# Key rows loaded from a second DMA queue, and eight row maxima moved to the end of the sequence before

## The chip, the cores and the metric

One Trainium2 chip, one of its cores. The metric is the device time of one execution, in microseconds; the time of the kernel before is the median of three runs. A profile shows one execution: its engines are TensorE (PE, with its weight loads PEld), VectorE (DVE), ScalarE (ACT), GpSimd (POOL), and the sequencers that issue DMAs, SyncE (SP) and ScalarE's (ACTq). 16 DMA engines move the data.

## What is computed

Two transformer layers on an input of 8 sequences of 512 rows of 128. The change lies in the first layer's part, which for each sequence is

```python
x = L0_attn_x
xn = _layernorm(x, axis=-1)
x = x + _L0_attn_ref(xn, ...) + _L0_ffn_ref(xn, ...)
```

where the attention has 16 heads of 8 dimensions, with keys and values from a latent of 32:

```python
q = (x @ W_q).reshape(b, t, N_HEADS, HEAD_DIM).transpose(0, 2, 1, 3)
k = (lat @ W_uk).reshape(b, t, N_HEADS, HEAD_DIM).transpose(0, 2, 1, 3)
v = (lat @ W_uv).reshape(b, t, N_HEADS, HEAD_DIM).transpose(0, 2, 1, 3)
q = apply_rope(q)
k = apply_rope(k)
scores = jnp.einsum('bhqd,bhkd->bhqk', q, k) / jnp.sqrt(jnp.float32(HEAD_DIM))
scores = jnp.where(causal[None, None], scores, -jnp.inf)
attn = jax.nn.softmax(scores, axis=-1)
```

and the FFN is a mixture of 32 experts (hidden 64, the best 4 of them) with a shared expert. The second layer, a gated delta rule with two mixtures of experts, is computed after it for all sequences in a loop of its own.

## The kernel before

Five engine programs are written out by hand and meet at semaphores. The first loop runs 8 times, once a sequence, and computes layer 1; the second runs 8 times for layer 2. The order of the first loop is the list that `schedule_l0` (L97) makes; each engine walks it and emits its own part of each step.

For one sequence the list is: `gu(p)` for p = 0 to 16, the gate and up products of a pair of experts (the 17th is the shared expert; TensorE L540, L543, ScalarE's Silu L973), `hid(p)`, VectorE's two products with the gate and the routing weight (L1361, L1364; `spread`, L532, gives the weight), and `wbd(p)`, the down product (L555). Between them stand the row maxima `max(n)`, n = 0 to 63, one for a head and a tile of 128 queries: TensorE multiplies the query rows with the key rows up to the diagonal (L570, 128 to 512 columns wide, `head_and_tile`, in banks 0 and 2 by turns), and VectorE adds the mask and reduces (L1372, behind a small waiting instruction, L326). n = 0, 1 are 128 wide, 2, 3 256, 4, 5 384, 6, 7 512, and so on in groups of eight. Six of them stand in each of the steps p = 2 and p = 3, four in each of p = 4 to 16. `maxneg` and `maxrows` turn the maxima of each half into rows that are stored, split in three bf16 parts, and loaded beside the query rows.

Then come the scores and exponentials `exp(g, i)` (L592, L597, ScalarE L982), 48 of them, the products with the values `pv(g)` (L610), numerator and denominator `nd` (L621), and `attn_out`: VectorE's reciprocal (L1394) and product (L1396), TensorE's output product (L628), VectorE's residual add, x1 (L1400). In between, the next sequence is prepared: `fnorm`, `fT`, `fq`, `flat`, `flatT`, `fk`, `fv`, `froute`, `fw` compute its normed input, queries, latent, keys, values and routing weights. What is prepared for the first sequence runs once ahead of the loop (`ahead_of_loop`).

Queries and keys are split in three bf16 parts each, stored to DRAM (`scratch_out`, L356, the scratch `scrq` and `scrk`) and loaded again in the layout that the products want (`scratch_in`, L365): the query rows QS and the key rows KS, each by 12 DMAs whose destination is 8 partitions x 8 x 512 bf16, 64 KB. All 24 are issued by SyncE, the queries' first, as soon as TensorE has done the last score of the running sequence, since QS and KS are read until then. TensorE waits for `d_q` and `d_k` ahead of maximum 0 (L565, L566), which stands in step p = 2 of the next sequence, behind gu(0) to gu(2). Behind the 24 loads SyncE stores x1 to `mid` (L396) and loads the next input.

After the loop VectorE waits for the last loads, which nothing uses, and clears XT (L1430); SyncE loads x1 of the first sequence back from `mid` (L401), and the second loop's first statistics start (L1218).

## Time and profile before

| | |
|---|---|
| median of 3 runs | 3121.79 us (3119.16 to 3141.93) |
| profiled execution | 3141.66 us, span 3139.9 us |
| granted TensorE clock, mean | 0.887 of 2.4 GHz |
| busy: PE, PEld, DVE, ACT, POOL | 86%, 58%, 65%, 38%, 12% |
| first loop in the span | about 62 to 1175 us |
| x1 (L1400), first and last of 8 | 216.2 and 1158.3 us |
| DMAs arena<-scrq, arena<-scrk | 108 and 108, 64 KB each |

"Busy" is an engine's share of the span; TensorE's matmuls are pipelined, so their busy time is not peak use. Per sequence the first loop takes 134.6 us ((1158.3-216.2)/7). Windows and timelines below are in us from the span's start; "[idle before <-releaser]" is the time that the engine stood still before the row and what it was released by. "DMA share" is the mean busy share of the 16 DMA engines.

### The profile page before, as it was taken

To read this page: it belongs to the slowest core of one execution; us is meant where nothing else is said; L and a number is where in the kernel's file an instruction comes from. 1 tells how busy PE (TensorE), PEld (TensorE's weight loads), DVE (VectorE), ACT (ScalarE), POOL (GpSimd) and SP (SyncE) were. 2 spreads that over 40 slices of the span, in tenths; PEclk is the share of its full clock that TensorE was granted. 3 is DMA by queue.
4 is the path that set the end of the run, shared out by engine and by line. 5 is a ranking of instruction groups with operands and counts; after the bars stand their busy time and mean duration, and the time that the engine had idled before them with its cause. 6 is when DMAs were issued, how large, how long until landed. Compare 5 with 4: busy or idle time off the path is not lost.

```text
span 3139.9 us, 48523 instructions
## 1 busy us (share of the span) xinstructions
PE 2691.1 (86%) x15020; PEld 1805.5 (58%) x15020; DVE 2042.6 (65%) x6346; ACT 1185.7 (38%) x2170; POOL 382.3 (12%) x284
## 2 busy tenths in 40 slices
PE   2888888888888867997997897898898898898898
PEld 1434343343433425784785685585596595586587
DVE  4757666585766748558558557657656756845845
ACT  0132231313223125445445444444444444544543
POOL 0000000000000002122112122021120220221211
PEclk8888878897898967998998998997998898899799
DMA  5020101102011121101101101101201201100110
GB/s 139 10 38 7 33 14 25 35 5 37 12 28 21 18 51 41 48 11 58 48 11 58 48 11 49 57 8 48 61 1 55 54 8 55 43 19 28 54 34 15
DMA packets 133697, 109.63 MB, mean 35 GB/s; under 512 B 76968, under 2 KB 117488, under 8 KB 132944
## 3 DMA queue, kind: packets, MB, share of 16 engines
q1 hardware_dynamic: 130192, 100.01, 12.7%
q10 hardware_dynamic: 3264, 6.82, 0.6%
q8 instruction: 100, 1.64, 0.2%
q14 instruction: 141, 1.16, 0.1%
HBM read 86.62 MB, written 20.19 MB: 34 GB/s over the span
## 4 chain that ended last, share of the span: by engine, by line
PE 62%; issue 18%; DVE 11%; DMA 3%; ACT 3%; SPq 2%; POOL 1%; DVEq 0%; ACTq 0%; POOLq 0%
PE bank L871 7%; PE bank L881 7%; PE bank L459 5%; DMA arena<-scrk 3%; DVE arena L1519 3%; PE bank L716 2%; PE bank L610 2%; PE bank L737 2%; PE bank L819 2%; PE bank L555 2%; PE bank L782 2%; PE bank L777 2%; PE bank L765 2%; PE bank L540 2%; PE bank L769 2%
## 5 line engine op out<-in xcount | busy, mean ns | idle before, releaser
L881 PEld LDWEIGHTS bank<-wring,arena 128*128 128x128 f32 x2048 | 269.1, 192 | 109.5 <-issue 107.2
L871 PE MATMUL bank<-arena,wring 128*128 128x512 f32 x512 | 294.8, 666 | 25.9 <-ACT arena L1100 25.9
L1100 ACT ACTIVATE arena<-bank,w_b 128x512 f32<-128x512 f32 x256 | 175.1, 687 | 274.2 <-PE bank L871 273.9
L1519 DVE SCALAR_TENSOR_TENSOR arena<-bank,w_convw,arena 128x511 f32<-128x511 f32 (+2 forms) x384 | 254.8, 740 | 34.6 <-ACT arena L1014 34.5
L881 PE MATMUL bank<-wring,arena 128*128 128x128 f32 x2048 | 271.1, 276 | 0.0
L973 ACT ACTIVATE arena<-bank 128x512 f32<-128x512 f32 x136 | 81.4, 599 | 494.7 <-PE bank L540 441.9
L459 PE MATMUL bank<-w_ident,arena 128*128 128x128 f32 (+2 forms) x1164 | 178.5, 293 | 86.4 <-DVE arena L1266 35.7
L1372 DVE CUSTOM_DVE_ANT_0 bank<-bank,arena 128x128 f32<-128x128 f32 (+3 forms) x512 | 249.2, 492 | 0.0
L982 ACT ACTIVATE arena<-bank 128x512 f32<-128x512 f32 (+1 forms) x384 | 171.1, 535 | 148.9 <-PE bank L597 147.1
L459 PEld LDWEIGHTS bank<-w_ident,arena 128*128 128x128 f32 (+2 forms) x1164 | 135.9, 141 | 118.6 <-issue 66.6
L692 PE MATMUL bank<-arena,w_Wqkvz 128*128 128x512 f32 x256 | 152.7, 733 | 45.0 <-DVE arena L1519 26.1
L1066 ACT ACTIVATE arena<-bank 128x512 f32<-128x512 f32 (+1 forms) x256 | 118.7, 488 | 136.2 <-PE bank L777 69.3
L570 PE MATMUL bank<-arena 48*128 48x128 bf16 (+3 forms) x512 | 110.7, 317 | 64.7 <-DVE arena L1372 36.0
L555 PE MATMUL bank<-arena 128*128 128x128 f32 x1088 | 161.7, 293 | 2.7 <-DVE arena L1357 2.7
L1684 DVE SCALAR_TENSOR_TENSOR arena<-bank,arena 128x128 f32<-128x128 f32 x224 | 63.1, 344 | 154.5 <-PE bank L881 152.7
L540 PE MATMUL bank<-arena 128*128 128x512 f32 x272 | 156.3, 659 | 8.1 <-ACT arena L973 8.1
L326 DVE TENSOR_TENSOR tick<-nhalf 128x1 f32<-128x1 f32 x600 | 94.1, 157 | 93.0 <-PE bank L570 86.4
L543 PE MATMUL bank<-arena 128*128 128x512 f32 x272 | 152.2, 644 | 0.0
L570 PEld LDWEIGHTS bank<-arena 48*128 48x128 bf16 x512 | 34.1, 93 | 200.5 <-DVE arena L1372 92.3
L555 PEld LDWEIGHTS bank<-arena 128*128 128x128 f32 x1088 | 135.6, 196 | 22.8 <-issue 11.3
L1175 POOL TENSOR_TENSOR arena<-arena,w_blk 128x512 f32<-128x512 f32 x64 | 79.8, 1268 | 509.5 <-PE bank L765 358.8
L1165 POOL TENSOR_TENSOR arena<-arena 128x512 f32<-128x512 f32 x64 | 92.3, 1475 | 352.2 <-ACT arena L1033 224.6
(273 smaller groups left out, 5209.3 us busy)
## 6 DMA issues: line engine op xcount, KB each, us to landing
wring<-in_w_last SPq DMA_DIRECT2D x64, 512.0 KB, 3.3
arena<-scrg SPq DMA_DIRECT2D x32, 512.0 KB, 5.4
arena<-scrq SPq DMA_DIRECT2D x108, 64.0 KB
arena<-scrk SPq DMA_DIRECT2D x108, 64.0 KB
scrn<-arena SPq DMA_DIRECT2D x64, 64.0 KB, 1.9
arena<-scrn SPq DMA_DIRECT2D x8, 512.0 KB, 3.6
scrx<-arena SPq DMA_DIRECT2D x8, 512.0 KB, 2.6
arena<-scrx SPq DMA_DIRECT2D x64, 64.0 KB, 2.1
```

What stands on the lines that cost most here:

```text
L459: return nc.tensor.transpose(dst, src, W["ident"][0:k, 0:k])
L540: mm(bk[:, :], W["gate0"][:, p, :] if p < PR0 else W["sg"][:], xnT, start=True, stop=True).then_inc(*s["p_gate"].up)
L543: mm(bk[:, :], W["up0"][:, p, :] if p < PR0 else W["su"][:], xnT, start=True, stop=True).then_inc(*s["p_up"].up)
L555: last = mm(bank[7][:, t * P:(t + 1) * P], HID[:, p % 2, t * P:(t + 1) * P], W["down0"][:, p, :] if p < PR0 else W["sd"][:], start=(p == 0 ...
L570: mm(bk[:, 0:w], QS[o:o + KROWS, h // 2, qt * P:(qt + 1) * P], KS[o:o + KROWS, h // 2, 0:w], start=True, stop=True, tile_position=(o, 0)). ...
L692: mm(bk[:, :], W["Wqkvz"][:, m * P:(m + 1) * P], zT, start=True, stop=True).then_inc(*s["p_qkv"].up)
L871: mm(bank[HBANK[f]][:, :], wring[:, e % 2, k * P:(k + 1) * P], xn1T, start=True, stop=True).then_inc(*s["p_fh"].up)
L881: last = mm(bank[OBANK[e]][:, t * P:(t + 1) * P], GH[:, f % 2, t * P:(t + 1) * P], wring[:, e % 2, FC * P + k * D:FC * P + (k + 1) * D], s ...
L982: fn(PT[:, slot, col:col + w], bank[SBANK[n % 4]][:, 0:w], ACT.Exp, scale=float(HD) ** -0.5).then_inc(*s["a_p"].up)
L1100: fn(GH[:, f % 2, :], bank[HBANK[f]][:, :], ACT.Gelu_apprx_tanh, bias=W["b1"][:, f:f + 1]).then_inc(*s["a_gh"].up)
L1372: v.tensor_tensor_reduce(bk[:, 0:w], bk[:, 0:w], W["maskq"][:, S - w:S], 1.0, PAD, ALU.add, ALU.max, mx[:, col:col + 1]).then_inc(*s["v_ma ...
L1519: ins = v.scalar_tensor_tensor(out=cv[:, k:S], in0=bank[2 + m % 4][:, 0:S - k], scalar=W["convw"][:, m, 3 - k:4 - k], in1=cv[:, k:S], op0= ...
```

## The change

It has three parts.

1. `scratch_in` on SyncE issues the 12 query loads only. The 12 key loads go to ScalarE's queue (`keys_in`), in the place of step `nd`, behind its last exponential, with the same waits.
2. Maxima 0 to 7 of the next sequence (`amax`, `AHEAD` = 8) are made at the end of this one: two between VectorE's product for the output and the output product, six behind the residual add. For the first sequence all eight are made ahead of the loop. The waits for `d_q` and `d_k` go with maximum 0, and `attn_out` is cut in two on VectorE (`att`, `attn_out`).
3. The other 56 maxima stand four in each of steps p = 2 to 15, from n = 8; the steps p = 2 and 3 have two fewer, p = 16 has none.

```diff
-    order, n = [("gu", 0)], 0
+    order, n = [("gu", 0)], AHEAD
     for p in range(1, PR0 + 1):
-        many = 0 if p == 1 else 6 if p in (2, 3) else 4
+        many = 0 if p in (1, PR0) else 4
...
-    order += [("pv", NQ - 1), ("nd",), ("attn_out",)]
+    order += [("pv", NQ - 1), ("nd",), ("att",), ("amax", 0), ("amax", 1), ("attn_out",)] + [("amax", i) for i in range(2, AHEAD)]
...
-                for name, scr, dst, kinds in (("q", scrq, QS, QSPLIT), ("k", scrk, KS, KSPLIT)):
-                    if name == "k":
-                        sp_.wait_ge(*s["d_scrk"].at(b, 32, k))
-                    for hh in range(2):
-                        for t, kind in enumerate(kinds):
...
+                for hh in range(2):
+                    for t, kind in enumerate(QSPLIT):
+                        rows = 64 * hh + HD * t
+                        sp_.dma_start(QS[rows:rows + HD, :, :], rows_of(scrq, kind, hh)).then_inc(*s["d_q"].up16)
...
+            def amax(b, k, n):
+
+                h, qt = head_and_tile(n)
+                o, w = 64 * (h % 2), P * (qt + 1)
+                if n == 0:
+                    pe.wait_ge(*s["d_q"].at(b, 16 * 12, k))
+                    pe.wait_ge(*s["d_k"].at(b, 16 * 12, k))
+                if k and n < 2:
+                    pe.wait_ge(*(s["v_os"].at(b, NQ), s["v_rden"].at(b, 1))[n])
+                if n >= 2:
+                    pe.wait_ge(*s["v_max"].at(b, n - 1, k))
+                mm(bank[(0, 2)[n % 2]][:, 0:w], QS[o:o + KROWS, h // 2, qt * P:(qt + 1) * P], KS[o:o + KROWS, h // 2, 0:w],
+                   start=True, stop=True, tile_position=(o, 0)).then_inc(*s["p_max"].up)
...
+            def keys_in(b, k):
+                if k:
+                    act.wait_ge(*s["p_score"].at(b, 12 * NQ))
+                act.wait_ge(*s["d_scrk"].at(b, 32, k))
+                for hh in range(2):
+                    for t, kind in enumerate(KSPLIT):
+                        rows = 64 * hh + HD * t
+                        act.dma_start(KS[rows:rows + HD, :, :], rows_of(scrk, kind, hh)).then_inc(*s["d_k"].up16)
...
+                         "nd": lambda: keys_in(b, 1)}
```

TensorE's rows where one sequence ends. Before, from the last products of `nd` (L621) over the output product (L628) to the loop's branch:

```order
L621 MATMUL bank<-arena 32x512 [waits v_os]
L621 MATMUL bank<-arena 32x512 x4
L628 MATMUL bank<-arena 128x128 [waits v_att]
L628 MATMUL bank<-arena 128x128 x3
L511 REGISTER_ALU
L511 COMPARE_AND_BRANCH
```

and, behind gu(0) and gu(1), the end of the wait's old place in the next turn of the loop, from gu(2) (L540, L543) to maximum 0 (L570):

```order
L540 MATMUL bank<-arena 128x512 [waits a_sg]
L516 ISA
L543 MATMUL bank<-arena 128x512 [waits v_t]
L565 ISA
L567 REGISTER_ALU [waits d_k,d_q]
L570 MATMUL bank<-arena 128x128 [waits v_att,v_os]
```

Now, with `nd` at L639, the maxima of `amax` at L524 and the output product at L646:

```order
L639 MATMUL bank<-arena 32x512 x4
L518 ISA
L524 MATMUL bank<-arena 128x128 [waits v_os,d_k,d_q]
L524 MATMUL bank<-arena 128x128 [waits v_rden]
L646 MATMUL bank<-arena 128x128 [waits v_att]
L646 MATMUL bank<-arena 128x128 x3
L523 REGISTER_ALU
L524 MATMUL bank<-arena 128x256 [waits v_max]
```

The wait for the loaded rows has moved from behind gu(2) of the next sequence to ahead of the output product, and six more maxima stand between that product and gu(0).

VectorE's rows there. Before, the reciprocal, the product, the residual add and the next sequence's first `hid` (L1361):

```order
L1394 RECIPROCAL arena<-bank 128x512 [waits p_nd]
L1258 REGISTER_ALU
L1395 REGISTER_ALU [waits v_tlink]
L1396 TENSOR_TENSOR arena<-bank,arena 128x512 [waits p_nd]
L1399 REGISTER_ALU [waits a_xr,p_acc]
L1400 TENSOR_TENSOR x<-arena,bank 128x512 [waits d_mid]
```

Now, with the same product at L1437, the maxima at L1380 and the residual add at L1443:

```order
L1437 TENSOR_TENSOR arena<-bank,arena 128x512 [waits p_nd]
L331 ISA
L332 TENSOR_TENSOR tick<-nhalf 128x1 [waits p_max]
L1380 ISA bank,arena<-bank,arena 128x128
L1380 ISA arena 128x1
L331 REGISTER_ALU
L332 TENSOR_TENSOR tick<-nhalf 128x1 [waits p_max]
L1380 ISA bank,arena<-bank,arena 128x128
L1380 ISA arena 128x1
L1442 REGISTER_ALU [waits a_xr,p_acc]
L1443 TENSOR_TENSOR x<-arena,bank 128x512 [waits d_mid]
L331 REGISTER_ALU
```

Two maxima have come ahead of the residual add, six stand behind it.

SyncE's rows at the same place, before:

```order
L376 DMA arena<-scrq 8x8x512 [waits p_score]
L376 DMA arena<-scrq 8x8x512 x11
L370 REGISTER_ALU
L376 DMA arena<-scrk 8x8x512 [waits d_scrk]
L376 DMA arena<-scrk 8x8x512 x11
L396 ISA [waits v_x1]
L396 DMA mid<-x 128x4x128
```

and now:

```order
L372 DMA scrk<-arena 128x512 [waits d_scrq]
L376 ISA
L380 DMA arena<-scrq 8x8x512 [waits p_score]
L380 DMA arena<-scrq 8x8x512 x11
L399 ISA [waits v_x1]
L399 DMA mid<-x 128x4x128
```

The key loads have left this queue; they are issued from ScalarE's, and the store to `mid` stands directly behind the query loads.

## Rows read from the trace of the kernel before

**Rows 1.** Who waited for whom, 62 to 1175 us: total, times, longest

```profile
PE bank L570 <- DMA arena<-scrk: 19.1, 5, 12.5
DVE arena L1430 <- issue: 10.5, 1, 10.5
```

**Rows 2.** Timeline, end of the fourth sequence: start, duration, engine, line

```profile
467.47 4.13 SPq L376 DMA_DIRECT2D arena<-scrq  x12
471.71 5.90 SPq L376 DMA_DIRECT2D arena<-scrk  x12
...
480.61 1.90 PE L628 MATMUL bank<-arena 128*128 128x128 f32 x8 [3.41 <-DVE arena L1396]
...
482.63 0.69 DVE L1400 TENSOR_TENSOR x<-arena,bank 128x512 f32<-128x512 f32 x1 [2.08 <-PE bank L628]
...
483.36 0.63 ACT L962 ACTIVATE arena<-arena 128x512 f32<-128x512 f32 x1 [15.01 <-DVE x L1400]
...
484.49 1.28 ACT L973 ACT_TABLE_LOAD   x1
...
486.44 1.13 PE L540 MATMUL bank<-arena 128*128 128x512 f32 x2 [1.29 <-ACT arena L973]
...
488.69 1.02 PE L540 MATMUL bank<-arena 128*128 128x512 f32 x2
...
493.55 0.23 PE L570 MATMUL bank<-arena 48*128 48x128 bf16 x2 [2.97 <-DMA arena<-scrk]
...
497.34 1.91 PE L540 MATMUL bank<-arena 128*128 128x512 f32 x2
```

**Rows 3.** Stretches: length, busy by engine, PEclk, DMA share, GB/s last

```profile
335.00:346.00 11.00, 8.20 (x80) 2.52 (x72) 4.18 (x3) 0.17 (x1) 0.00 (x0) 0.89 0.56 85
468.50:481.00 12.50, 8.27 (x78) 2.75 (x71) 5.43 (x4) 0.00 (x0) 0.00 (x0) 0.91 0.57 71
484.00:488.00 4.00, 2.71 (x7) 1.08 (x6) 0.69 (x1) 2.75 (x4) 0.00 (x0) 0.97 0.95 126
3.00:11.00 8.00, 0.00 (x0) 0.00 (x0) 0.00 (x0) 0.00 (x0) 0.00 (x0) 1.00 1.01 403
...
468.00:469.00 1.00, 1.00 (x8) 0.20 (x4) 0.00 (x0) 0.35 (x2) 0.00 (x0) 0.50 0.35 100
```

**Rows 4.** Timeline of VectorE, maxima of the fifth sequence

```profile
495.55 0.43 DVE L1372 CUSTOM_DVE_ANT_0 bank<-bank,arena 128x256 f32<-128x256 f32 x1
...
497.25 0.56 DVE L1372 CUSTOM_DVE_ANT_0 bank<-bank,arena 128x384 f32<-128x384 f32 x1
```

**Rows 5.** Timeline of TensorE, gate products of gu(2), gu(4), gu(5), gu(6)

```profile
355.47 1.02 PE L540 MATMUL bank<-arena 128*128 128x512 f32 x2
...
365.37 1.02 PE L540 MATMUL bank<-arena 128*128 128x512 f32 x2
...
369.39 1.02 PE L540 MATMUL bank<-arena 128*128 128x512 f32 x2
...
372.90 1.02 PE L540 MATMUL bank<-arena 128*128 128x512 f32 x2
```

**Rows 6.** Timeline of TensorE, first and last down product of a sequence's end

```profile
420.43 1.16 PE L555 MATMUL bank<-arena 128*128 128x128 f32 x8
...
424.43 1.16 PE L555 MATMUL bank<-arena 128*128 128x128 f32 x8 [0.34 <-DVE arena L1357]
```

**Rows 7.** Timeline, first sequence: SyncE's query loads, TensorE's gu(4)

```profile
61.50 4.25 SPq L376 DMA_DIRECT2D arena<-scrq  x12
...
98.78 1.02 PE L540 MATMUL bank<-arena 128*128 128x512 f32 x2
```

**Rows 8.** Timeline of VectorE, end of the first loop

```profile
1158.26 0.69 DVE L1400 TENSOR_TENSOR x<-arena,bank 128x512 f32<-128x512 f32 x1 [1.94 <-PE bank L628]
...
1169.49 3.47 DVE L1430 MEMSET arena<- 128x4096 f32 x1 [10.54 <-issue]
...
1173.02 0.80 DVE L1218 BATCH_NORM_STATS2 stats<-x 128x6 f32<-128x128 f32 x4
```

More of the change, by code:

```diff
@@ L192, in sig @@
             if first:
-                signals[name] = Signal(name, signals[first].sem, per.get(name, 1), (LOOPS + (first in FRONT)) * per.get(first, 1))
+                signals[name] = Signal(name, signals[first].sem, per.get(name, 1), (LOOPS + (first in FRONT)) * per.get(first, 1) + PARTLY.get(first, 0))
             else:
@@ L508, in fw, with first_maxima @@
                 last.then_inc(*s["p_w0T"].up)
-            ahead_of_loop(fT, fq, flat, flatT, fk, fv, fw)
+            def amax(b, k, n):
[10 more added lines that the diff above has]
+                   start=True, stop=True, tile_position=(o, 0)).then_inc(*s["p_max"].up)
+            def first_maxima(b, k):
+                for n in range(AHEAD):
+                    amax(b, k, n)
+            ahead_of_loop(fT, fq, flat, flatT, fk, fv, fw, first_maxima)
             with pe.Fori(0, LOOPS) as b:
@@ L563, in smax @@
                     o, w = 64 * (h % 2), P * (qt + 1)
-                    if n == 0:
-                        pe.wait_ge(*s["d_q"].at(b, 16 * 12))
-                        pe.wait_ge(*s["d_k"].at(b, 16 * 12))
+                    if n == AHEAD:
                         pe.wait_ge(*s["v_os"].at(b, 0))
-                        pe.wait_ge(*s["v_att"].at(b, 0))
-                    bk = after(*(("v_nmt", 1) if n == 32 else ("v_max", max(n - 1, 0))), (0, 2)[n % 2])
+                    bk = after(*(("v_nmt", 1) if n == 32 else ("v_max", n - 1)), (0, 2)[n % 2])
                     mm(bk[:, 0:w], QS[o:o + KROWS, h // 2, qt * P:(qt + 1) * P], KS[o:o + KROWS, h // 2, 0:w],
@@ L634, in _ @@
                          "attn_out": attn_out, "fT": later(fT), "fq": later(fq), "flat": later(flat), "flatT": later(flatT),
-                         "fk": later(fk), "fv": later(fv), "fw": later(fw)}
+                         "fk": later(fk), "fv": later(fv), "fw": later(fw), "amax": lambda n: amax(b, 1, n)}
                 for step in L0:
@@ L982, in expo @@
                     fn(PT[:, slot, col:col + w], bank[SBANK[n % 4]][:, 0:w], ACT.Exp, scale=float(HD) ** -0.5).then_inc(*s["a_p"].up)
-                steps = {"gu": gu, "exp": expo, "fT": lambda: fT(b, 1), "flatT": lambda: flatT(b, 1)}
+                steps = {"gu": gu, "exp": expo, "fT": lambda: fT(b, 1), "flatT": lambda: flatT(b, 1),
+                         "nd": lambda: keys_in(b, 1)}
                 for step in L0:
@@ L1345, in _, with row_max, amax, first_maxima @@
             ahead_of_loop(fnorm, fq, flat, flatT, fk, froute, fw)
+            def row_max(n):
+                h, qt = head_and_tile(n)
+                w, col = P * (qt + 1), h * NT + qt
+                bk = bank[(0, 2)[n % 2]]
+                v.tensor_tensor_reduce(bk[:, 0:w], bk[:, 0:w], W["maskq"][:, S - w:S], 1.0, PAD,
+                                       ALU.add, ALU.max, mx[:, col:col + 1]).then_inc(*s["v_max"].up)
+            def amax(b, k, n):
+                wait_alone(dve, *s["p_max"].at(b, n + 1, k))
+                row_max(n)
+            def first_maxima(b, k):
+                for n in range(AHEAD):
+                    amax(b, k, n)
             def dve_steps(b, k):
@@ L1367, in smax @@
                 def smax(n):
-                    h, qt = head_and_tile(n)
-                    w, col = P * (qt + 1), h * NT + qt
                     wait_alone(dve, *s["p_max"].at(b, n + 1, k))
-                    bk = bank[(0, 2)[n % 2]]
-                    v.tensor_tensor_reduce(bk[:, 0:w], bk[:, 0:w], W["maskq"][:, S - w:S], 1.0, PAD,
-                                           ALU.add, ALU.max, mx[:, col:col + 1]).then_inc(*s["v_max"].up)
+                    row_max(n)
                 def maxneg(half):
@@ L1403, in dve_steps @@
                 later = lambda part: lambda: part(b, k + 1)
[L1404 to L1405 removed]
+                return {"hid": hid, "max": smax, "maxneg": maxneg, "maxrows": maxrows, "pv": pv, "att": attend, "attn_out": attn_out,
+                        "amax": lambda n: amax(b, k + 1, n), "fnorm": later(fnorm), "fq": later(fq), "flat": later(flat), "flatT": later(flatT), "fk": later(fk),
                         "froute": later(froute), "fw": later(fw)}
```

25 lines of the change are left out of this document (12 added, 13 removed).

## Prediction

> **What bounds the kernel now.** I read the views in this order: who waited for whom over the first loop, then one end of a sequence as a timeline, then the DMA share there, then the pace of the steps that the change shortens.
>
> The second loop is untouched and only shifts. In the first loop, which runs from about 62 to 1175 us of the span, TensorE is paced by itself, by VectorE and by three fixed chains. Only 19.1 us of its time wait for key rows, 12.5 of them once, ahead of the first sequence, and 6.6 in four of the seven others [rows 1]. VectorE waits another 10.5 us for the last, unused keys after the loop [rows 1]. So 29.6 us in all is what the loads cost openly. They take much longer than that. In the fourth sequence's end SyncE issues 12 query loads from 467.47 (call this moment S), then 12 key loads from 471.71, and the first maximum starts at 493.55, S+26.1, after 2.97 us of waiting [rows 2]. Everything TensorE does between 480.61 and about 490 (the output product, the first gate and up products of the next sequence, gu(0) to gu(2)) lies over these loads.
>
> Issue is not what takes the time: the 24 issues are over at 477.6, 16 us before the data is there [rows 2]. The loads run at a steady 71 GB/s here and 85 GB/s in another sequence, at a DMA share of 0.57 and 0.56, that is about nine of sixteen engines' worth [rows 3]. When the next input and the stored result join on the same queue, the share goes to 0.95 and the rate to 126 GB/s; the start of the kernel shows 403 GB/s at a share of 1.01 [rows 3]. So there are engines left over that these loads don't use, and each load that is in flight is slow.
>
> **The change part by part.** Call L the landing of the last key row, counted from S. Everything turns on L, because the wait for it moves from ahead of the old first maximum (about S+23 to S+26) to ahead of the output product, which starts at 480.61, S+13.1, now [rows 2].
>
> 1. *What now stands behind the wait.* New order on TensorE: maxima 0 and 1, output product, maxima 2 to 7, then gu(0). The matmuls of maxima 0 and 1 take 0.2 and their wake 0.1, the output product 1.9 [rows 2], so it ends at L+2.2. VectorE then does the residual add, 0.69 [rows 2], and the maxima: one 256 wide is 0.41 after the one before, one 384 wide 0.55, and the 512 wide ones 0.69 each by the same rate per column (an estimate from the 0.43 and 0.56 of the rows), with a gap of about 0.3 at each change of width (an estimate from 495.55 and 497.25, which lie 1.7 apart where three maxima take 1.4) [rows 4]. The six maxima behind the add are 3.3 us of VectorE and 0.7 of such gaps, 4.0: it is through at L+7.1. TensorE needs maximum 5 for the last matmul, about L+5.5, and gu(0) follows. ScalarE's two copies and its table load (1.28) [rows 2] run in that time. gu(0), its activation of 0.6 and the start of gu(1) are at L+7.8, where before gu(1) came 3.9 after the output product's end, at 486.44 [rows 2]. gu(2) follows 2.3 later: L+10.1, against 488.69, S+21.2. Cost of this part: L-11.1.
>
> 2. *What the FFN steps give back.* Before, the two steps after gu(2) hold six maxima each and take 9.9 us where nothing waits (355.47 to 365.37); a step with four wide ones takes 4.0, one with four narrow ones 3.5 [rows 5]. Now all fourteen steps hold four, which makes these two 7.5: 2.4 gained. On top goes the open wait for keys, 6.6/7 = 0.95 a sequence, and what follows it: after the idle time the clock is granted at half and the next product takes 1.91 instead of 1.02 [rows 2]; I put 0.75 on that. The last step now has no maxima: the three down products, 1.16 each, can run back to back instead of ending at 425.6 after starting at 420.43; with the small transpose that is 3.8 instead of 5.2 plus 0.5 that maxnegs and waits add: 1.9 gained [rows 6]. Sum: 2.4+0.95+0.75+1.9 = 6.0.
>
> 3. *Between two sequences*, seven times: L-11.1-6.0 = L-17.1.
>
> 4. *The first sequence.* Query loads are issued at 61.50, the keys need their store landed and start about 2 us later instead of 4. The eight maxima stand alone, 4.2 to gu(0), then 4.8 to gu(2) and 7.5 to gu(4): 61.5+(L+1)+16.5 against 98.78 [rows 7]; and 1.9 less at the last step.
>
> 5. *The end of the loop.* VectorE clears XT (3.47) once the maxima are through: the statistics start at L+10.8 in place of 1173.02. The x1 of that sequence is at 1158.26, which is S+15.2 there, so S is about 1143.1 and the old value S+29.9 [rows 8].
>
> ScalarE's 12 issues cost nothing: it idles 15.01 us ahead of the copy that follows x1, and at SyncE's pace of 5.9 us for twelve [rows 2] they are over by S+7. Without that cover they would cost these 6 us. SyncE has nothing else queued until x1. The banks of maxima 0 and 1 are free before the output product could start, so they hold nothing up.
>
> *How large is L?* No row shows two queues on such loads. 24 loads of 64 KB are 1.57 MB. **If a second queue adds nothing**, 85 to 71 GB/s give 18.5 to 22.2 us, and the packets begin about 1.1 after S (the microsecond from 468 has them only in its second half, at a share of 0.35) [rows 3]: L = 19.6 to 23.3. **If it doubles the rate**, the loads are in by S+13.1 and the output product waits for nothing: L = 13.1. I take 90 GB/s, a little over the best that one queue shows, nearer to the lower end because the share of 0.57 says that the engines which serve these loads are busy all the time: L = 18.6.
>
> Sum at L = 18.6: 7 x 1.5 = +10.5; first sequence 97.6-98.78-1.9 = -3.1; end 29.4-29.9 = -0.5. Together +7 us. On the profiled execution (3141.66 us, span 3139.9) that is 3149; on the median of the runs, 3121.79, it is 3129. The profiled run is 20 us above that median; the difference is not the loads', and I forecast the median.
>
> The Trainium skill (DMA: Bandwidth & Descriptors, "Issuing engines are not separate DMA queues") says that DMAs from several engines run on the same 16 DMA engines and interleave, and that only issue time is saved. By it the time would be that of the rival "nothing gained" below. The same skill (SBUF, "Door 1: The DMA port swizzle") has eight neighbouring partitions behind two of sixteen ports; by that, query rows and key rows in flight on different ports could run side by side, which speaks for the rival "doubled".
>
> **The rivals.**
>
> *Nothing gained (slower).* The wait of L = 19.6 to 23.3 now stands ahead of the output product and all of gu(0) to gu(2), 10 us of TensorE's work that lay over it. For: the share of 0.57 is unchanged between the 71 and the 85 GB/s sequence, so the serving engines look full. Against: their rate differs by a fifth between sequences, so they are not at a hard limit. Price: at 19.6, 17.5-2.1+0.5 = +16; at 23.3, 43.4+1.6+4.2 = +49: 3138 to 3171. It decides on slower at all from L = 17.1, and on slower by 1% from L = 21.2.
>
> *Doubled (faster).* L = 13.1: 7 x -4.0 = -28; first sequence 92.1-98.78-1.9 = -8.6; end -6.0: -43, 3079. For: sixteen engines carry 403 GB/s, these loads 71. At L = 14.2 it is still -32.
>
> *Shared in part*, my forecast: L from 14.2 to 19.6, 3090 to 3138.
>
> A fourth, that ScalarE's issues delay its copies, I leave at 2 in 100: they would have to take 10 us longer.
>
> **How the numbers follow.** Shared in part 0.41, nothing gained 0.33, doubled 0.24, else 0.02. One per cent, 31 us, is about what a measurement of this kernel can tell from no change. Faster by over 1% needs L under 14.2: the doubled case and a little, 0.26. Slower by over 1% needs L over 21.2: most of the second, 0.27. Within: 0.47. The range 3082 to 3168 leaves a tenth out at each end; the likeliest case alone is 3090 to 3138.
>
> **What the profile would show.** L: the idle time of the first maximum's matmul, put down to the key rows, now ahead of the output product; with L = 18.6 it is 5.4 us a sequence. The rate in the first 15 us after S: 71 to 85 GB/s for nothing gained, 140 for doubled. gu(1) 5.6 after the output product. The steps 4.0 and 3.5 from gu(2) on. The forecast falls if the output product still starts at S+13, or if the rate stays at 71.

## The result, and the profile after

| | before | after |
|---|---|---|
| median of four runs each, same chip | 3126.78 us | 3179.93 us |
| ratio, 95% interval | | 1.017 (1.012 to 1.0219) |
| profiled execution, span | 3139.9 us | 3174.5 us |
| second loop's first statistics start | 1173.02 us | 1224.54 us |
| from one sequence's query loads to the next's, mean of seven | 134.6 us | 141.3 us |

The changed kernel is slower by 53 us, and its median lies 12 us above the upper end of the range (3168). The forecast was 3129. The first loop alone holds the loss: the second loop's statistics start 51.5 us later than in [rows 8]. The spans of the two profiled executions lie only 34.6 us apart because the second loop, which is the same in both, took 17 us more in the execution of before. Over the thirteen kernels told of here the time from VectorE's clearing of XT to the end runs from 1954 to 1977 us with the same code, so for the first loop I compare its end and use the ratios for the whole.

The page of the changed kernel, its busy times, the chain that ended last, and the group of the early maxima:

```profile
PE 2647.2 (83%) x15028; PEld 1788.4 (56%) x15028; DVE 2045.4 (64%) x6370; ACT 1184.4 (37%) x2170; POOL 382.0 (12%) x284
...
PE 60%; issue 18%; DVE 10%; DMA 6%; ACT 3%; POOL 2%; SPq 1%; DVEq 0%; ACTq 0%; POOLq 0%
```

Its waits in the first loop, 62 to 1230 us (total, times, longest): ScalarE for x1, TensorE at the first early maximum, VectorE for the early maxima, and TensorE there once more:

```profile
ACT arena L990 <- DVE x L1443: 182.8, 7, 26.7
...
PE bank L524 <- DMA arena<-scrq: 116.1, 8, 15.8
DVE tick L332 <- PE bank L524: 107.1, 24, 12.8
...
PE bank L524 <- DMA arena<-scrk: 15.9, 1, 15.9
```

TensorE stood 19.1 us at the key rows in [rows 1]. Now it stands 132.0 us at the loaded rows (116.1 + 15.9), nine times, the longest 15.9. (Eight of the waits are put down to the query loads. The profile names the transfer that came last by its reckoning, and in the eight loads inside the loop queries and keys land within 0.4 us of each other. In the first load, ahead of the loop, the keys are 5.2 us behind.) DMA is 6% of the chain.

The same end of the fourth sequence as in [rows 2], as a timeline of the changed kernel:

```profile
483.79 4.12 SPq L380 DMA_DIRECT2D arena<-scrq  x12
...
483.88 0.27 ACTq L984 DMA_DIRECT2D arena<-scrk  x1
...
484.18 3.93 ACTq L984 DMA_DIRECT2D arena<-scrk  x11
...
506.41 0.29 PE L524 MATMUL bank<-arena 48*128 48x128 bf16 x2 [13.05 <-DMA arena<-scrq]
506.63 2.07 PE L646 MATMUL bank<-arena 128*128 128x128 f32 x8
...
508.83 0.69 DVE L1443 TENSOR_TENSOR x<-arena,bank 128x512 f32<-128x512 f32 x1 [1.41 <-PE bank L646]
...
509.55 0.63 ACT L990 ACTIVATE arena<-arena 128x512 f32<-128x512 f32 x1 [25.00 <-DVE x L1443]
...
512.55 2.04 PE L561 MATMUL bank<-arena 128*128 128x512 f32 x2
...
516.09 1.63 PE L561 MATMUL bank<-arena 128*128 128x512 f32 x2
...
518.85 1.02 PE L561 MATMUL bank<-arena 128*128 128x512 f32 x2
522.36 1.02 PE L561 MATMUL bank<-arena 128*128 128x512 f32 x2
526.39 1.03 PE L561 MATMUL bank<-arena 128*128 128x512 f32 x2
```

S is 483.79. Both queues have issued their twelve loads by S+4.3 instead of S+10.1, and still the first maximum starts at S+22.6. TensorE stands idle for 13.05 us, from S+9.6 to S+22.6. Before, it stood idle for the first 3.41 us of that and ran the output product and gu(0) to gu(2) in the rest. Stretches of the changed kernel in two sequences, and behind the wait (length, busy by engine, PEclk, DMA share, GB/s):

```profile
486.00:504.00 18.00, 6.53 (x72) 2.07 (x64) 5.43 (x4) 0.00 (x0) 0.00 (x0) 0.78 0.57 77
345.00:363.00 18.00, 5.30 (x56) 1.52 (x48) 5.44 (x4) 0.00 (x0) 0.00 (x0) 0.74 0.57 71
...
506.00:519.00 13.00, 11.13 (x27) 5.29 (x28) 5.82 (x27) 3.60 (x5) 0.00 (x0) 0.57 0.14 40
```

The DMA share with two queues is 0.57, the number of [rows 3] with one, and the rate is 77 and 71 GB/s. The last row is what comes behind the idle time: TensorE is granted 0.57 of its 2.4 GHz on average, so much of the stretch is at the lower level of 1.2 GHz, and gu(0) takes 2.04 where it takes 1.02 at full clock.

### The profile page after: what moved, and what is told of

It reads as the page before. It is cut to its first block, busy times and chain, and to the rows that moved or that the text cites. A ratio compares the mean times of both kernels' runs of the same rounds, so it can differ in the third digit from the quotient of the medians.

```text
span 3174.5 us, 48555 instructions
## 1 busy us (share of the span) xinstructions
PE 2647.2 (83%) x15028; PEld 1788.4 (56%) x15028; DVE 2045.4 (64%) x6370; ACT 1184.4 (37%) x2170; POOL 382.0 (12%) x284
## 3 DMA queue, kind: packets, MB, share of 16 engines
q1 hardware_dynamic: 122416, 92.93, 10.8%
## 4 chain that ended last, share of the span: by engine, by line
PE 60%; issue 18%; DVE 10%; DMA 6%; ACT 3%; POOL 2%; SPq 1%; DVEq 0%; ACTq 0%; POOLq 0%
PE bank L889 7%; PE bank L899 7%; DMA arena<-scrq 5%; PE bank L462 4%; DVE arena L1562 4%; PE bank L561 3%; PE bank L564 2%; PE bank L837 2%; PE bank L576 2%; PE bank L755 2%; PE bank L800 2%; PE bank L795 2%; PE bank L783 2%; PE bank L787 2%; PE bank L856 2%
## 5 line engine op out<-in xcount | busy, mean ns | idle before, releaser
L1562 DVE SCALAR_TENSOR_TENSOR arena<-bank,w_convw,arena 128x511 f32<-128x511 f32 (+2 forms) x384 | 253.9, 736 | 25.0 <-ACT arena L1043 21.6
L1380 DVE CUSTOM_DVE_ANT_0 bank<-bank,arena 128x128 f32<-128x128 f32 (+3 forms) x520 | 253.1, 492 | 0.0
L462 PE MATMUL bank<-w_ident,arena 128*128 128x128 f32 (+2 forms) x1164 | 172.0, 286 | 74.3 <-DVE arena L1295 35.5
L710 PE MATMUL bank<-arena,w_Wqkvz 128*128 128x512 f32 x256 | 148.9, 719 | 43.7 <-DVE arena L1562 26.1
L524 PE MATMUL bank<-arena 48*128 48x128 bf16 (+3 forms) x72 | 25.0, 442 | 144.3 <-DMA arena<-scrq 116.1
L576 PEld LDWEIGHTS bank<-arena 128*128 128x128 f32 x1088 | 133.9, 194 | 18.6 <-issue 12.1
L1043 ACT ACTIVATE arena<-bank,w_convw 128x512 f32<-128x512 f32 x128 | 87.6, 685 | 107.8 <-PE bank L710 107.4
```

The lines of the kernel that those rows point to most:

```text
L462: return nc.tensor.transpose(dst, src, W["ident"][0:k, 0:k])
L576: last = mm(bank[7][:, t * P:(t + 1) * P], HID[:, p % 2, t * P:(t + 1) * P], W["down0"][:, p, :] if p < PR0 else W["sd"][:], start=(p == 0 ...
L710: mm(bk[:, :], W["Wqkvz"][:, m * P:(m + 1) * P], zT, start=True, stop=True).then_inc(*s["p_qkv"].up)
L1380: v.tensor_tensor_reduce(bk[:, 0:w], bk[:, 0:w], W["maskq"][:, S - w:S], 1.0, PAD, ALU.add, ALU.max, mx[:, col:col + 1]).then_inc(*s["v_ma ...
L1562: ins = v.scalar_tensor_tensor(out=cv[:, k:S], in0=bank[2 + m % 4][:, 0:S - k], scalar=W["convw"][:, m, 3 - k:4 - k], in1=cv[:, k:S], op0= ...
```

## The experiments

L is, as in the prediction, the landing of the last key row counted from the issue of the first query load. It is worked out for each of the nine loads of a kernel from the issue rows and the landing times in the trace. "Spacing" is the mean distance from one S to the next over the seven inner sequences; "clear" is the start of VectorE's clearing of XT at the end of the first loop. The ratios are to the kernel before on the same chip, with their 95% intervals.

| kernel | L of the first, of the others | spacing | clear | ratio |
|---|---|---|---|---|
| before | 26.1, 21.7 to 25.7 | 134.6 | 1169.5 | 1 |
| changed | 22.8, 22.5 to 24.2 | 141.3 | 1221.0 | 1.017 (1.012 to 1.0219) |
| two_queues_old_order | 23.9, 23.6 to 25.4 | 136.6 | 1179.6 | 0.9991 (0.9958 to 1.0024) |
| one_queue | 25.8, 21.6 to 26.3 | 141.4 | 1226.4 | 1.0139 (1.0069 to 1.021) |
| before_wide | 13.0, 12.4 to 13.1 | 133.1 | 1136.9 | 0.9881 (0.982 to 0.9941) |
| after_wide | 12.9, 13.1 to 13.6 | 130.3 | 1126.7 | 0.98 (0.9757 to 0.9843) |
| after_wide_one_queue | 14.2, 12.2 to 13.5 | 130.2 | 1125.5 | 0.9796 (0.9753 to 0.9839) |
| wait_behind | 22.6, 22.2 to 25.7 | 140.5 | 1211.8 | 1.0102 (1.0052 to 1.0152) |
| before_wide_even | 13.5, 11.9 to 13.3 | 133.1 | 1138.4 | 0.9867 (0.9818 to 0.9916) |
| other_half | 27.6, 15.6 to 20.2 | 136.0 | 1183.4 | 0.999 (0.9957 to 1.0022) |
| other_rows | 24.2, 16.5 to 21.9 | 137.0 | 1190.2 | 1.0052 (1.002 to 1.0085) |
| sixteen_rows | 15.4, 16.0 to 16.4 | 133.2 | 1150.2 | 0.9956 (0.9923 to 0.9989) |
| eight_rows | 24.2, 26.0 to 28.1 | 143.9 | 1246.4 | 1.0219 (1.0155 to 1.0284) |

### Which part of the change costs

**two_queues_old_order**: the kernel before, with `keys_in` on ScalarE's queue and nothing else.

```diff
-                for name, scr, dst, kinds in (("q", scrq, QS, QSPLIT), ("k", scrk, KS, KSPLIT)):
+                for name, scr, dst, kinds in (("q", scrq, QS, QSPLIT),):
...
+            ahead_of_loop(fT, flatT, keys_in)
```

> The kernel before, with the key loads on ScalarE's queue and nothing else changed: the wait for them stands behind gu(2) of the next sequence as before. Theory A: the time of the kernel before within 0.5%, 3110 to 3140 us; the last row lands 22 to 24.5 us after the first issue and TensorE's wait ahead of maximum 0 is 10 to 30 us in all. Theory B: slower by over 20 us. A landing at 13 to 17 us would give 3090.

**one_queue**: the changed kernel, with all 24 loads back on SyncE's queue.

```diff
+                sp_.wait_ge(*s["d_scrk"].at(b, 32, k))
+                for hh in range(2):
+                    for t, kind in enumerate(KSPLIT):
+                        rows = 64 * hh + HD * t
+                        sp_.dma_start(KS[rows:rows + HD, :, :], rows_of(scrk, kind, hh)).then_inc(*s["d_k"].up16)
...
-            ahead_of_loop(fT, flatT, keys_in)
+            ahead_of_loop(fT, flatT)
...
```

> The changed kernel, but all 24 loads issued by SyncE again, queries first; the maxima stay where the change put them. Theory A (the landing of the last key row does not depend on the number of queues; moving the wait ahead of the output product is the whole loss): the last row lands 21.7 to 26 us after the first query load's issue as in the kernel before, against 22.5 to 24.2 in the changed one, so the time is that of the changed kernel within 0.5%, about 3170 to 3190 us. Theory B (two queues in lockstep slow each other, and the queue split is part of the loss): faster than the changed kernel by over 20 us, 3150 or less. If the queue split had gained anything, this kernel would be slower than 3190.

The second queue alone changes nothing that can be measured in the ratio (0.9991), and taking it away from the changed kernel changes nothing either (1.0139 and 1.017, intervals that overlap widely). The mean L of the seven inner loads is 23.2 and 24.2 in the old order, 24.0 and 23.7 in the new one, with one queue and with two. So the loss lies in the place of the wait. One thing does not fit as well: in the profiled execution of two_queues_old_order a sequence takes 136.6 us against 134.6, and the first loop ends 10.1 us later, which the ratio does not show. Stretches of one_queue, to be put beside the 77 and 71 GB/s above (the first begins 1.2 us ahead of its S, 487.20; from 488.50 to 504 it is 0.57 and 77):

```profile
486.00:504.00 18.00, 9.58 (x86) 2.94 (x84) 5.75 (x5) 2.04 (x6) 0.00 (x0) 0.81 0.51 70
345.00:363.00 18.00, 7.82 (x80) 2.36 (x72) 5.43 (x4) 0.00 (x0) 0.00 (x0) 0.78 0.57 68
```

In two_queues_old_order TensorE's wait for the keys becomes eight waits and not five, 23.2 us in all against 19.1, because L is 24 to 25 in every sequence and not about 22 in four of them:

```profile
PE bank L568 <- DMA arena<-scrk: 23.2, 8, 10.1
```

### Is the new order bad, or only L too long for it?

**before_wide** and **after_wide**: the kernel before and the changed kernel with another layout in the scratch, 48 rows of 16 heads, so that each tensor comes back in two transfers of 48 partitions instead of twelve of eight. The stores become six a tensor, of 128 KB. Of the edit, the loads of before_wide:

```diff
-                    for hh in range(2):
-                        for t, kind in enumerate(kinds):
-                            rows = 64 * hh + HD * t
-                            part = bass.AP(tensor=scr.tensor, offset=kind * P * S + hh * HD * S,
-                                           ap=[[S, HD], [2 * HD * S, NP], [1, S]])
-                            sp_.dma_start(dst[rows:rows + HD, :, :], part).then_inc(*s["d_" + name].up16)
+                    for hh in range(2):
+                        sp_.dma_start(dst[64 * hh:64 * hh + KROWS, :, :], wide_rows(scr, hh)
+                                      ).then_inc(*s["d_" + name].up16)
...
```

> The kernel before, with a scratch of 48 rows (six parts of eight, three of them stored twice or more) so that each half of QS and KS is loaded by one DMA of 48 partitions, 4 loads in place of 24, all from SyncE; the pieces stay 1 KB and the bytes loaded stay the same, the stores grow from 3 to 12. Both theories E and P: the loads run on all sixteen DMA engines and all ports of a half, the rate is 250 GB/s or more, the last row lands within 6 to 9 us, and no matmul waits for it. Then the 19.1 us of TensorE's waits, some 5 us of half clock behind them and 8 of the 10.5 us at the loop's end go: 3085 to 3100 us. If instead the limit were the memory read (small pieces from one small region), it would still take 20 us and the time would be that of the kernel before.

> The changed kernel with nothing altered but the scratch layout and the load shape: each tensor comes back in 2 transfers of 48 partitions instead of 12 of eight. In the kernel before, this shape brought L (landing of the last key row, counted from the issue of the first query load) down to 12.4 to 13.1 us. By the prediction's own sum with L = 12.7: seven sequences L - 17.1 = -4.4 us each, -31; first sequence about -6; end of loop 23.5 instead of 29.9, -6; together about -43 us against the kernel before, ratio 0.986, and some 5 us under before_wide. Theory A (the change's order is sound and only the load's length spoilt it): ratio 0.984 to 0.988, no wait of more than 2 us on the keys in the loop. Rival B (the order itself costs, whatever the load's length, because eight maxima and the output product now stand in the end of the sequence): slower than before_wide (0.988) by 3 us or more.

For before_wide an L of 6 to 9 us was expected, at 250 GB/s or more. It came to 12.4 to 13.1 us, at 139 GB/s. Still its wait at the maxima is gone but for 1.9 us once, ahead of the first sequence, and every spacing is 133.1. The ratio of after_wide lies where theory A has it, and a little under (0.98 for 0.984 to 0.988), and rival B is out: spacing 130.3, first loop 42.8 us shorter than in the profiled execution of before ("about -43"). TensorE's waits ahead of the early maxima in after_wide, 62 to 1230 us:

```profile
PE bank L528 <- issue: 25.0, 6, 5.3
...
PE bank L528 <- DMA arena<-scrk: 8.9, 1, 8.9
...
PE bank L528 <- DMA arena<-scrq: 7.6, 2, 4.0
```

16.5 us in three pieces are put down to the loads, 8.9 of them once, and the other two are longer than the 2 us that theory A allowed. Those two and the six of 25.0 us stand where the old order had 3.41 of idle time ahead of each output product [rows 2], until VectorE's product is there. In the fourth sequence of after_wide the keys land at S+13.5, 466.8, and the first maximum starts at 466.90; VectorE's product had ended at 466.15. So L is still what releases TensorE, but by 0.7 us there. Over the eight loads of the loop the keys land 0.0 to 0.8 us behind the end of that product, and 1.9 in one, and a shorter L would bring little more than that.

So the order is not bad in itself. With L at 13 it is 2.8 us a sequence better than the old one, with L at 24 it is 6.7 worse. (Over the whole first loop after_wide is 10.2 us ahead of before_wide in the profiled executions, and after_wide_one_queue, below, 11.4; the intervals of the ratios 0.98 and 0.9881 overlap.) after_wide beats both kernels of this study, by 2.0% and 3.6% (0.98/1.017).

The seven spacings are not the whole of it. At the same L the first sequence and the end of the loop cost more in the new order, since nothing lies over the loads there: from the first S to the second it is 127.9 us in after_wide and 123.9 in before_wide, from the last S to the clearing of XT 21.5 and 16.6.

**after_wide_one_queue**: the same four wide loads, all from SyncE.

```diff
+                sp_.wait_ge(*s["d_scrk"].at(b, 96, k))
+                for hh in range(2):
+                    sp_.dma_start(KS[64 * hh:64 * hh + KROWS, :, :], wide_rows(scrk, hh)).then_inc(*s["d_k"].up16)
...
```

> As after_wide, with the four wide loads all from SyncE's queue. If two queues working on the same rows of SBUF gain nothing (as one_queue against the changed kernel showed for eight-partition loads), L and the time are those of after_wide within 0.3%. If wide loads leave the queues something to share, L is longer here by 1 us or more than in after_wide, and the time by 8 us or more.

0.9796 against 0.98: with wide transfers too the second queue gains nothing. Stretches from the middle of the loads, one queue (after_wide_one_queue) and then two (after_wide):

```profile
456.00:465.00 9.00, 6.08 (x68) 1.87 (x60) 4.30 (x3) 0.00 (x0) 0.00 (x0) 0.99 1.08 139
```

```profile
456.00:465.00 9.00, 5.98 (x68) 1.87 (x60) 4.40 (x3) 0.00 (x0) 0.00 (x0) 1.00 1.11 138
```

**wait_behind**: the changed kernel with the output product ahead of all eight early maxima.

```diff
-    order += [..., ("att",), ("amax", 0), ("amax", 1), ("attn_out",)] + [("amax", i) for i in range(2, AHEAD)]
+    order += [..., ("att",), ("attn_out",)] + [("amax", i) for i in range(AHEAD)]
```

> The changed kernel (eight-partition loads) with one thing moved: the output product stands ahead of all eight early maxima instead of behind the first two, so that the wait for the keys comes behind the output product. Theory P (the wait's end, L = 24 us, is what the sequence waits for, and the eight maxima take their 6 us behind it either way): the next sequence's first pair starts at the same time within 1 us, the ratio to the kernel before is that of the changed kernel (1.017) less 0 to 0.3%. Rival Q (the loss is that the output product and the chain through the residual, the normalised rows and its transposes stand behind the wait): about 5 us of each sequence come back, ratio 1.002 to 1.006.

Spacing less L is 115.7 here and 117.6 in the changed kernel: 1.9 us a sequence come back by moving the output product, but L is a microsecond longer in this execution (24.7 against 23.7 in the mean), and half is left, 0.9 us a sequence. The clearing of XT starts 9.2 us earlier. The ratio, 1.0102 (1.0052 to 1.0152), lies between what theory P and rival Q had (1.014 to 1.017, and 1.002 to 1.006), and its interval reaches into both. P had gu(0) start at the same time within 1 us. From S it does, in the fourth sequence (S+29.6 against S+28.8), but behind an L that is 2.6 us longer there, and counted from L it starts 1.8 us earlier (L+4.5 against L+6.2). Q had about 5 us a sequence. So the output product's place is a part of the loss, and a small one. The timeline has what limits it: the eight maxima have to stand behind the wait in either order and take 4.4 us from the first to gu(0), here as a chain between TensorE and VectorE with nothing beside it.

```profile
505.35 0.29 PE L524 MATMUL bank<-arena 48*128 48x128 bf16 x2 [10.22 <-DMA arena<-scrq]
...
509.73 2.04 PE L561 MATMUL bank<-arena 128*128 128x512 f32 x2
```

**before_wide_even**: before_wide with four maxima in each step from 1 to 16.

```diff
-        many = 0 if p == 1 else 6 if p in (2, 3) else 4
+        many = 4
```

> The kernel before with the wide loads, and the maxima spread evenly: four behind each of the 16 gate and up pairs 1 to 16, none of the steps of six. The wait for the keys moves from behind the pair 2 to behind the pair 1, about S + 17.7 us. Theory: L = 12.8 is over by then, so nothing waits, and two steps of 9.9 fall to 7.5 while one of about 3.6 grows to 7.5: -0.9 us in each of eight sequences, -7 us against before_wide, ratio about 0.986. Rival: the first sequence and the last pay for it (the keys stand on the path there, about 3.6 us less cover), so that 0 to -4 us are left.

The evening out gains nothing: spacing 133.1 as in before_wide, and 0.9867 against 0.9881. Its loads come early enough (L 12.5 is over ahead of the first maximum), so this is no wait. From S (the SyncE rows of before_wide and of this kernel) the gate product of gu(4) starts 31.1 us later in before_wide (454.74, 485.86) and 30.6 in this one (456.21, 486.84), so 0.5 of the expected 0.9 was there at that point. At gu(12) it is still 0.5 (S+66.9 against S+66.4), at gu(16) 0.1 (S+84.0 against S+83.9), and by the next S it is gone. The runs don't show what takes it back.

### Why L is 24 us, and why a second queue does not shorten it

**other_half**: the changed kernel with the keys' half of partitions 64 to 111 loaded first, while SyncE loads the queries' half 0 to 47.

```diff
-                for hh in range(2):
+                for hh in (1, 0):
```

> The changed kernel, with the key loads in the order rows 64 to 111 first, rows 0 to 47 second, so that the two queues never write neighbouring partitions at the same time (in the changed kernel both go through the same eight rows in step). Theory P (what limits them is the eight partitions that both queues write at a time): the rate doubles from 68 to 110 to 135 GB/s, the last row lands at 13 to 16 us, and by 7 x (L - 17.1) and the two ends the time is 3080 to 3115 us. Theory E (what limits them is the part of the DMA engines that a load with an outermost dimension of eight uses, whatever it writes): no change, 3170 to 3190 us, share still near 0.5.

**other_rows**: the changed kernel with the six key transfers of a half in another order, so that both queues write the same half but never the same eight partitions at a time.

```diff
-                    for t, kind in enumerate(KSPLIT):
-                        rows = 64 * hh + HD * t
+                    for t in (3, 4, 5, 0, 1, 2):
+                        kind, rows = KSPLIT[t], 64 * hh + HD * t
```

> The changed kernel with the six key transfers of each half in the order 3, 4, 5, 0, 1, 2, so that at no time the two queues write the same eight partitions of their buffers, but both write the same half (partitions 0 to 47, then 64 to 111). Theory same-rows (the two queues block each other by writing the same eight partitions at a time): L falls from 24 to the 16 to 20 us of other_half, ratio 0.998 to 1.002. Rival same-half (what counts is that they write the same half of the partitions): L stays at 23 to 25 us, ratio 1.015 to 1.02. By the spacing of the sequences in the runs so far (L + 117.3 us), each microsecond of L is 8 us of the total.

Both shorten L, to 18.6 and 19.5 in the mean of the seven inner loads (15.6 to 20.2 and 16.5 to 21.9, against 22.5 to 24.2 in the changed kernel), though the first load of a run stays at 24 to 28. Neither theory for other_half held whole: the share stayed near 0.5, as E had it, and L fell, as P had it, but to 18.6 and not to 13 to 16. Different rows of the same half do nearly as much as the other half, so rival same-half is out, though the ratio of other_rows, 1.0052, lies outside what either side had. Two stretches of other_half and two of other_rows:

```profile
476.00:490.00 14.00, 5.79 (x68) 1.77 (x60) 5.43 (x4) 0.00 (x0) 0.00 (x0) 0.86 0.57 85
342.00:352.00 10.00, 6.04 (x64) 1.94 (x56) 5.23 (x4) 0.00 (x0) 0.00 (x0) 0.97 0.57 115
```

```profile
480.00:492.00 12.00, 6.42 (x68) 1.96 (x60) 5.43 (x4) 0.00 (x0) 0.00 (x0) 0.93 0.57 109
344.00:358.00 14.00, 6.04 (x68) 1.94 (x60) 5.43 (x4) 0.00 (x0) 0.00 (x0) 0.87 0.57 96
```

The share is 0.57 in all of them, and the rate at that share goes from 71 and 77 GB/s in the changed kernel to 85 to 115. My reading is that the engines that serve these loads were busy in every case, and that what a second queue can change is only how fast each of them gets its bytes off. With both queues starting 0.09 us apart and walking the same list, the changed kernel wrote the same eight partitions of its two buffers at about the same time, which is the case that gains nothing. Two things stay open. Both orders also shift which part of the scratch is read beside which, and no run separates what is read from what is written. And with one queue, too, the rate moves at this share (71 and 85 GB/s in [rows 3], L from 21.6 to 26.3 in one_queue), for which no run has the cause.

**sixteen_rows** and **eight_rows**: after_wide with its transfers cut into three of sixteen partitions, or into six of eight.

```diff
-                    act.dma_start(KS[64 * hh:64 * hh + KROWS, :, :], wide_rows(scrk, hh)).then_inc(*s["d_k"].up16)
+                    for r in range(0, KROWS, 16):
+                        act.dma_start(KS[64 * hh + r:64 * hh + r + 16, :, :], wide_rows(scrk, hh, r)).then_inc(*s["d_k"].up16)
...
```

The query loads are cut in the same way, and eight_rows has 8 in the place of 16.

> after_wide with each transfer of 48 partitions cut into three of sixteen (6 transfers a tensor, both queues), same scratch layout, same order. In the changed kernel the transfers of eight partitions kept the DMA engines busy at a share of 0.57 whether one queue or two issued them, and the 48-partition ones at 1.1. Theory engines (a transfer's rows are dealt out over as many of the 16 engines as it has partitions, up to 16): sixteen partitions are enough, share about 1.1 while they run, L 13 to 15, ratio 0.980 to 0.984. Rival partitions (what counts is how many partitions are written together): share 1.1 but rate well under the 139 GB/s of after_wide, L 17 to 20, ratio 0.99 to 1.0.

> after_wide with each transfer of 48 partitions cut into six of eight: the transfers of the changed kernel, on the new scratch layout. If the shape of the transfer is the whole of it, L is again 22 to 25 us, the share 0.57 and the ratio 1.012 to 1.02, as in the changed kernel. Rival (the scratch layout helped too, since a transfer's source is now one contiguous run of rows): L under 20 us and the ratio under 1.0.

Stretches of sixteen_rows and of eight_rows:

```profile
464.50:475.00 10.50, 5.08 (x48) 1.51 (x48) 5.43 (x4) 0.00 (x0) 0.00 (x0) 0.94 1.15 112
```

```profile
498.00:520.00 22.00, 6.09 (x68) 1.94 (x60) 5.43 (x4) 0.00 (x0) 0.00 (x0) 0.73 0.57 65
```

Sixteen partitions take the share from 0.57 to 1.15 and L from 26.6 to 16.2: twice the engines. The traces bear this out in a second way. For a load of eight partitions its semaphore is updated nine times (972 times for 108 loads), once right behind the issue, before any data, and eight times as the data lands. For a load of sixteen or 48 partitions it is sixteen times (864 for 54 loads of sixteen). That is all of the share, but not all of the rate. 112 GB/s is under the 139 of the 48-partition transfers, L lies between the two theories' numbers, and the ratio 0.9956 is the rival's side of them. So the engines count first, and something more is gained beyond sixteen partitions. Whether that is the width or the smaller number of transfers (four in place of twelve), no run separates. eight_rows has the new layout and the old transfers, and its L is 26 to 28 and its ratio 1.0219, both above what was expected and above the changed kernel's: the layout did nothing for after_wide, the larger transfers did all. (Its twelve issues also take 8.8 and 9.1 us a queue where those of the changed kernel take 4.1 and 4.2. The reason is open.)

The Trainium skill (DMA: Bandwidth & Descriptors, "Why a DMA increments its semaphore by 16 and not by 1") has the number of engines of a transfer follow from its slowest dimension, the largest number up to 16 that divides it on both sides of the transfer: eight for these loads. The shares agree, 0.57 at eight partitions and 1.15 at sixteen.

## Why the prediction was wrong, step by step

**The size of L failed, and nothing else of weight.** The step was "I take 90 GB/s, a little over the best that one queue shows, nearer to the lower end because the share of 0.57 says that the engines which serve these loads are busy all the time". The reason given speaks for no gain at all, and the runs show none: L was 23.7 in the mean of the inner loads against 18.6 in the forecast, and 24 in one_queue and two_queues_old_order. I held against this rival that the rate differs by a fifth between sequences, "so they are not at a hard limit". The runs show that the rate can move at a constant share of 0.57, in one_queue with a single queue and in other_half and other_rows with the rows that two queues write together. So a rate that differs between sequences was no sign of room for a second queue on this list of loads.

**The upper end of L was also short.** 23.3 came from the 1.57 MB at 71 GB/s. The sequence of [rows 2] already shows S+26.1, and L in that trace runs from 21.7 to 26.1: the range should have taken that. With the mean of its seven inner loads, 23.2, the prediction's own sum gives 42.7+1.5+4.1 = +48, or 3170. One more number of the working is off: "slower at all from L = 17.1" holds between two sequences, while by its own sum the first sequence and the end give 6.6 us back at that L, so that slower at all begins at 17.8.

**Steps 1 to 3, L-17.1 a sequence: right.** That is a spacing of 134.6+L-17.1 = L+117.5. Spacing less L, in the mean of the seven, is 117.6 in the changed kernel, 117.4 in one_queue, 117.4, 117.5, 116.9 and 117.2 in other_half, other_rows, sixteen_rows and eight_rows, and 116.9 and 117.5 in the two wide ones: from L = 12.7 to L = 26.6 the same line (in the wide kernels L is hardly what TensorE waits for, and they fit all the same). Against a sequence of the old order that waits for nothing, 133.1, the new order breaks even at L = 15.7. Over the whole first loop it breaks even earlier. From the first S to the clearing of XT it is 1072.3 us in before_wide, 1061.2 in after_wide at L = 13.3 and 1086.0 in sixteen_rows at L = 16.2, which puts it at about 14.6, an estimate by a straight line between the last two. other_half ran at L = 18.6, the forecast's own value: spacing 136.0, where the forecast has 136.1, and a ratio of 0.999.

**Inside that sum two terms were off and cancelled.** Step 1: from the end of the wait (506.41) to gu(2) (518.85) it is 12.4 us, forecast 10.1. Of the 2.3 us, 0.6 came ahead of gu(0) (+6.1 for +5.5), 1.2 between gu(0) and gu(1) (+9.7 for +7.8 in all), and the rest ahead of gu(2). What was missed is the granted clock behind a wait of 13 us, with gu(0) at 2.04 and gu(1) at 1.63. The trace of before had a sign of it, since gu(0) took 1.91 there behind only 3.41 us of idle time:

```profile
482.30 1.91 PE L540 MATMUL bank<-arena 128*128 128x512 f32 x2
```

Step 2: from gu(2) of this sequence to the S of the next it is 104.7 us (518.85 to 623.55), where an unwaited sequence of before took 112.0 (355.47 in [rows 5] to 467.47 in [rows 2]): 7.3 given back, forecast 2.4+1.9 = 4.3 without the two terms for waits. The two steps of six gave 2.4 (9.9 to 7.54, gu(2) to gu(4)), as said. From the last step's gate product to the first score products it is 7.9 us instead of 10.3, 2.4 against the 1.9 forecast. The other 2.5 us lie in small pieces over the other steps and the exponentials, and I can't put them down to one cause; before_wide_even shows that evening out the steps is not by itself a gain.

**Step 4, the first sequence: right in form.** gu(4) starts at 103.27 in the changed kernel. The forecast for L = 22.8 is 61.5+23.8+16.5 = 101.8. S itself came 1.0 late there. By the next S the sequence is 0.8 us ahead of the kernel before (200.24 against 201.06), where the sum at this L has it 1.1 behind.

**Step 5, the end of the loop: right.** The statistics start at L+11.4 (1189.52+23.6, 1224.54), forecast L+10.8.

**The sum at the measured L.** 7 x (23.7-17.1) = +46, first sequence +1, end of the loop 34.4-29.9 = +4.5, together +52; measured +51.5 at the start of the second loop's statistics, and +53 in the medians. That the total fits to a microsecond is in part luck: the three terms measured +47.0, -0.8 and +5.3, each 1 to 2 us off. But the slope of about nine us for each of L is right, and the error of 5.1 us in L is nearly all of the miss.

**ScalarE's issues cost nothing: right.** They run beside its last exponentials (484.18), and its wait for x1 grew from 15.01 to 25.00. But the keys started 0.09 us behind the queries, which put both queues in step on the same rows.

**The sign for the wait was mis-sized.** It had 5.4 us of idle time a sequence at L = 18.6. It left out the 3.41 us that TensorE stands there in any case [rows 2]: other_half, at that L, has 75.7 us in eight, 9.5 each.

**The rivals.** *Nothing gained* is what happened, with the mechanism that its text names, and it had 0.33. The rule of the Trainium skill that stood beside it (DMA: Bandwidth & Descriptors, "Issuing engines are not separate DMA queues") agrees with the runs of one queue against two, at eight partitions in step and at 48. It does not tell of other_half, where two queues on different rows had L at 18.6 against 24.0 in one_queue; one queue with such an order was not run. *Doubled* did not come, but its time did once L was 13: 3079 forecast, a ratio of 0.986; after_wide ran at 0.98. What the Trainium skill has on ports (SBUF — State Buffer, "Door 1: The DMA port swizzle") was no reason for it here, since both queues wrote the same rows at a time, and other_rows shows what different rows are worth: 4 us of L.

## What to carry to other kernels

When a wait is moved forward, price it as a line in the landing time of what is waited for, and measure that landing time before the move: here each microsecond of it costs about nine over the loop (97.4 us from after_wide to the changed kernel, for 10.3 of L), and a sequence wins below 15.7 us and loses above, the whole loop below about 14.6. A DMA share that stands still at about one half while loads run was here the sign of transfers that use half of the engines. Then a second queue, with the keys issued 4.2 us earlier, brought nothing on the same rows and 4 to 5 us of L on different ones, and wider transfers brought 7 to 11. Give the transfer a wider partition dimension first, and change the order after.

## What the runs showed of the hardware that I had not expected

- Transfers of 8 partitions ran at a DMA share of 0.57 with one queue and with two, of 16 partitions at 1.15, of 48 at 1.1. The rates were 60 to 85 GB/s at eight partitions (both tensors' loads in step, or from one queue), 112 at sixteen and 139 at 48.
- At the same share of 0.57 the rate rose from 71 and 77 to between 85 and 115 GB/s when the two queues wrote different partitions at a time, whether of the same half of the buffers or of the other. The first load of these runs gained nothing (24.2 and 27.6). In every first load with two queues the keys are issued 1.8 to 2.0 us behind the queries and not 0.09; whether that is the reason no run shows.
- Behind 13 us of idle time with nothing to multiply, TensorE's granted clock was 0.57 of 2.4 GHz in the mean over the next 13 us, although the products of that stretch kept it busy for 11.1 of them.
